# A graph layer's prologue on Trainium2: four groups of four tiles become eight pairs of tiles

## The reference, cut to what matters

```python
h = maximum(layernorm(x), 0)                       # (2048, 256)
type_sum = adj @ h
gate_a = sigmoid(concat([type_sum, h]) @ Wa.T + ba)  # one number per node; gate_b with Wb, bb
g = h @ W_sa
scores = (g @ a_sa[:D])[:, None] + (g @ a_sa[D:])[None, :]
e = where(adj != 0, exp(-leaky_relu(scores, 0.01)), 0)
x_a = e / (e.sum(1) + 1e-5) @ g
x_b = adj @ (h @ W_gcnb) + b_gcnb
return x + sigmoid(gate_a * x_a + gate_b * x_b)
```

## Time and profile before

| what | us |
|---|---|
| median of three runs | 194.56 |
| the profiled execution | 194.4 |
| its span, first to last instruction | 192.6 |
| TensorE busy | 172.1 (89%) |
| VectorE busy | 143.6 (75%) |
| ACT busy | 114.3 (59%) |
| GpSimd busy | 16.1 (8%) |

### The profile page before, as it was taken

How to read it: one execution, slowest core, us unless ns; L and a number is a source line. 1 busy time by engine, 2 the same in 40 slices (tenths; PEclk the granted TensorE clock), 3 DMA queues, 4 the chain that set the end, 5 groups by cost and what they waited for, 6 DMA issues and landing times.

```text
span 192.6 us, 3345 instructions
## 1 busy us (share of the span) xinstructions
PE 172.1 (89%) x1320; PEld 127.0 (66%) x1320; DVE 143.6 (75%) x289; ACT 114.3 (59%) x166; POOL 16.1 (8%) x34
## 2 busy tenths in 40 slices
PE   0348968687999999999999999999999999999993
PEld 0326554455544444588887446888888888888893
DVE  0647574436789999937999993099999999987641
ACT  0285747554489998860947574057587587592421
POOL 1371403302400020000000000000000000000000
PEclk9999999999999999999999999999999999999999
DMA  5999995695000039800000100000001001010210
GB/s 149 404 203 207 213 216 109 109 218 114 3 0 0 0 49 214 175 0 0 3 0 2 58 37 18 0 3 0 0 3 54 0 21 38 2 58 0 93 47 27
DMA packets 3615, 13.72 MB, mean 71 GB/s; under 512 B 400, under 2 KB 784, under 8 KB 2704
## 3 DMA queue, kind: packets, MB, share of 16 engines
q0 software_dynamic: 1296, 8.39, 22.4%
q1 hardware_dynamic: 2016, 4.20, 5.9%
q10 hardware_dynamic: 288, 0.93, 1.4%
HBM read 19.80 MB, written 2.10 MB: 114 GB/s over the span
## 4 chain that ended last, share of the span: by engine, by line
PE 82%; ACT 7%; DMA 3%; DVE 2%; issue 2%; POOL 2%; SPq 0%; DVEq 0%
PE ps L713 23%; PE ps L737 15%; PE ps L738 15%; PE ps L736 15%; PE ps L688 7%; PE ps L729 5%; DMA x_sb<-in_x 3%; ACT scratch L272 3%; PE ps L676 2%; ACT nat_hi L277 1%; ACT scratch L284 1%; PE ps L698 1%; DVE mv_lo L473 1%; DVE scratch L454 1%; ACT mv_hi L295 1%
## 5 line engine op out<-in xcount | busy, mean ns | idle before, releaser
L736 PE MATMUL ps<-mv_lo,e_hi 128*128 128x257 f16 (+2 forms) x272 | 71.0, 267 | 0.0
L738 PE MATMUL ps<-mv_hi,e_lo 128*128 128x257 f16 (+2 forms) x272 | 70.9, 266 | 0.0
L737 PE MATMUL ps<-mv_hi,e_hi 128*128 128x257 f16 (+2 forms) x272 | 70.8, 266 | 0.0
L312 ACT ACTIVATE scratch<-scratch,log_e 128x1024 f32<-128x1024 f32 x32 | 36.7, 1146 | 27.2 <-DVE scratch L499 27.2
L713 PE MATMUL ps<-adj,nat_hi 128*128 128x512 f16 x128 | 48.5, 379 | 0.0
L713 PE MATMUL ps<-adj,nat_lo 128*128 128x512 f16 x128 | 48.5, 379 | 0.0
L499 DVE SCALAR_TENSOR_TENSOR scratch<-sl_row,exs,scratch 128x512 f32<-128x512 f32 x64 | 45.0, 745 | 0.0
L507 DVE TENSOR_TENSOR e_lo<-scratch,e_hi 128x1024 f16<-128x1024 f32 x32 | 39.0, 1219 | 1.2 <-ACT e_hi L320 1.2
L320 ACT ACTIVATE e_hi<-scratch 128x1024 f16<-128x1024 f32 x32 | 33.3, 1041 | 0.0
L737 PEld LDWEIGHTS ps<-mv_hi,e_hi 128*128 128x128 f16 x272 | 26.6, 98 | 3.2
L736 PEld LDWEIGHTS ps<-mv_lo,e_hi 128*128 128x128 f16 x272 | 26.4, 97 | 3.3
(11 more groups left out here) (61 smaller groups left out, 166.4 us busy)
## 6 DMA issues: line engine op xcount, KB each, us to landing
adj<-in_adj_t POOLq DMA_DIRECT2D x7, 1024.0 KB, 12.7
x_sb<-in_x SPq DMA_DIRECT2D x4, 512.0 KB, 7.1
out<-res SPq DMA_DIRECT2D x7, 256.0 KB, 2.0
adj<-in_adj_t POOLq DMA_DIRECT2D x2, 512.0 KB, 7.8
w_sb<-in_weights ACTq DMA_DIRECT2D x1, 518.0 KB, 5.2
c_sb<-in_consts ACTq DMA_DIRECT2D x1, 387.0 KB, 5.9
out<-res SPq DMA_DIRECT2D x1, 128.0 KB, 1.8
out<-res SPq DMA_DIRECT2D x2, 64.0 KB, 1.5
```

The source lines that it names most:

```text
L312: act.activation(z[:, n % ZRING, :, :], z[:, n % ZRING, :, :], ACT.Exp, bias=log_e[:, 0:1], scale=SLOPE - 1.0).then_inc(exp_done, 1)
L736: pe.matmul(ps[:, bank, cols], e_hi[:, s, i1], mv_lo[:, j, cols], start=(j == 0), stop=False)
L737: pe.matmul(ps[:, bank, cols], e_hi[:, s, i1], mv_hi[:, j, cols], start=False, stop=False)
L738: return pe.matmul(ps[:, bank, cols], e_lo[:, s, i1], mv_hi[:, j, cols], start=False, stop=(j == NT - 1))
```

## The change

The prologue goes over eight pairs of tiles (`u`) instead of four groups, and every engine's order is a loop that does the steps of different pairs in turn. TensorE: turn of pair u+1, wide of u, chunk 0's products of pair u. The wide results alternate between banks 2, 3 and 6, 7, the turned pairs between banks 0 and 1. h0 is written over x in place; x is loaded a second time from memory when all turns and low parts are done, for the sum at the end. ACT makes the row scale directly by an exp with a bias, in place of an exp and a GpSimd multiply. x comes in five pieces, the first two of two tiles; all of x, constants and weights are issued by SP; the weights and constants are split in two each, the wide weights ahead of the rest of x. VectorE makes both parts of the wide weights. Sixteen matmuls on zeros stand at the head of TensorE's queue. The turned tiles and the zeros lie in slots of the e ring. The row turns for chunks 2 and 3 go into the middle of chunk 1's products. `half_added` on ACT waits for the second load of x, `agg_highs(0)` stands one step earlier, and the split of the post weights (`w_post_low`) stands between the prologue and the loop on VectorE.

The core of the diff:

```diff
+NU = NT // 2
+WARM = 16
+X_PARTS = ((0, 2), (2, 4), (4, 8), (8, 12), (12, 16))
+WIDE_BANKS = (2, 6)
...
+        h0t_hi = e_hi[:, 16:24, :].rearrange("p (k s) n -> p k (s n)", k=KT)
+        h0t_lo = e_lo[:, 16:24, :].rearrange("p (k s) n -> p k (s n)", k=KT)
+        zeros = e_hi[:, 0, :]
+        z = sb("z", [P, ZRING, 2, CW], F32)
+        far = sb("far", [P, 2, 2, CW], F16)
...
+        def turn_bank(u):
+            return ps[:, u % 2, :].rearrange("p (k n) -> p k n", k=KT)
...
+            def load_x(i):
+                lo, hi = X_PARTS[i]
+                sp.dma_start(x_sb[:, lo:hi, :], x[:, lo:hi, :]).then_inc(x_landed[i], 16)
+
+            load_x(0)
+            load_x(1)
+            sp.dma_start(c_sb[:, :], consts).then_inc(c_landed, 16)
+            sp.dma_start(wa_sb[:, :, :], w_wide).then_inc(wa_landed, 16)
+            for i in range(2, len(X_PARTS)):
+                load_x(i)
+            sp.dma_start(wg_sb[:, :, :], w_post).then_inc(wg_landed, 16)
+            sp.dma_start(r_sb[:, :], rows).then_inc(rows_landed, 16)
+            sp.wait_ge(turned, NU)
+            sp.wait_ge(nat_ready, NU)
             for g in range(NG):
-                sp.dma_start(x_sb[:, g * GT:(g + 1) * GT, :], x[:, g * GT:(g + 1) * GT, :]).then_inc(x_landed[g], 16)
+                ts = slice(g * GT, (g + 1) * GT)
+                sp.dma_start(x_sb[:, ts, :], x[:, ts, :]).then_inc(x_back[g], 16)
...
+            def norms(u):
+                ts = slice(2 * u, 2 * u + 2)
+                pool.wait_ge(var_ready, u + 1)
                 pool.tensor_tensor(rstd[:, ts], var_s[:, ts], power[:, :], ALU.pow).then_inc(rstd_ready, 1)
-                pool.wait_ge(rstd_ready, g + 1)
+                pool.wait_ge(rstd_ready, u + 1)
                 pool.tensor_tensor(shift[:, ts], neg_mean[:, ts], rstd[:, ts], ALU.mult).then_inc(norm_ready, 1)
...
-            pool.wait_ge(x_landed[1], 16)
+            pool.wait_ge(x_landed[0], 16)
             load_adj(0)
             norms(0)
+            norms(1)
             load_adj(1)
-            norms(1)
+            norms(2)
+            norms(3)
             load_adj(2)
+            norms(4)
             load_adj(3)
-            norms(2)
+            norms(5)
             load_adj(4)
-            scales(0)
-            norms(3)
-            scales(1)
+            norms(6)
+            norms(7)
             load_adj(5)
             load_adj(6)
-            scales(2)
-            scales(3)
-            pool.tensor_scalar(column[:, :], factor_r[:, :], MV_SCALE, None, ALU.mult).then_inc(column_done, 1)
+            pool.wait_ge(scales_ready, NU)
...
-            act.dma_start(c_sb[:, :], consts).then_inc(c_landed, 16)
-            act.wait_ge(x_landed[0], 16)
-            act.dma_start(w_sb[:, :, :], weights).then_inc(w_landed, 16)
-
...
+            def h0_tiles(u):
+                act.wait_ge(norm_ready, u + 1)
+                for t in range(2 * u, 2 * u + 2):
+                    act.activation(x_sb[:, t, :], x_sb[:, t, :], ACT.Relu, bias=shift[:, t:t + 1],
                                    scale=rstd[:, t:t + 1]).then_inc(h0_done, 1)
 
...
+            def nat_highs(u):
+                ts = slice(2 * u, 2 * u + 2)
+                act.wait_ge(h0_done, 2 * u + 2)
+                act.activation(nat_hi[:, ts, :], x_sb[:, ts, :], ACT.Copy).then_inc(nat_high, 1)
+
+            def h0t_highs(u):
+                act.wait_ge(turned, u + 1)
+                act.activation(h0t_hi[:, :, 2 * u * P:(2 * u + 2) * P], turn_bank(u),
+                               ACT.Copy).then_inc(h0t_high, 1)
+
+            def mv_highs(u):
+                act.wait_ge(exs_ready, u + 1)
+                act.activation(scale_a[:, 2 * u:2 * u + 2], exs[:, 2 * u:2 * u + 2, SR], ACT.Exp, bias=log_s[:, 0:1],
+                               scale=-SLOPE).then_inc(scales_ready, 1)
+                act.wait_ge(scales_ready, u + 1)
+                for t in range(2 * u, 2 * u + 2):
+                    act.activation(mv_hi[:, t, 0:D], ps[:, WIDE_BANKS[u % 2] + t % 2, 0:D], ACT.Copy,
                                    scale=scale_a[:, t:t + 1]).then_inc(mv_high, 1)
...
+                elif n == 8:
+                    act.wait_ge(wide_product, NT)
...
+                act.wait_ge(x_back[g], 16)
...
+            act.wait_ge(wl_product, 1)
+            act.wait_ge(wa_landed, 16)
+            act.activation(wa_sb[:, :, D:D + 2], wl_bank, ACT.Copy).then_inc(wl_ready, 1)
             h0_tiles(0)
-            act.wait_ge(wl_product, 1)
-            act.wait_ge(w_landed, 16)
-            act.activation(w_sb[:, :, D:D + 2], wl_bank, ACT.Copy).then_inc(wl_ready, 1)
-            act.wait_ge(wl_ready, 1)
-            act.activation(w_hi[:, :, 0:WA], w_sb[:, :, 0:WA], ACT.Copy, scale=W_SCALE).then_inc(w_high, 1)
             h0t_highs(0)
+            h0_tiles(1)
             nat_highs(0)
-            h0_tiles(1)
-            h0t_highs(1)
-            nat_highs(1)
-            factors(0)
-            h0_tiles(2)
-            mv_highs(0)
+            act.wait_ge(consts_ready, 1)
+            for u in range(NU):
+                if u + 1 < NU:
+                    h0t_highs(u + 1)
+                if u + 2 < NU:
+                    h0_tiles(u + 2)
+                if u + 1 < NU:
+                    nat_highs(u + 1)
+                mv_highs(u)
+            act.activation(factor_l[:, :], exs[:, :, SL], ACT.Exp, scale=SLOPE).then_inc(factors_done, 1)
             sl_rows(0)
-            h0t_highs(2)
-            nat_highs(2)
-            factors(1)
-            h0_tiles(3)
-            mv_highs(1)
             sl_rows(1)
-            h0t_highs(3)
-            nat_highs(3)
-            factors(2)
-            mv_highs(2)
-            act.activation(w_hi[:, :, WA:], w_sb[:, :, WA:], ACT.Copy, scale=W_SCALE).then_inc(w_high, 1)
-            factors(3)
-            sl_rows(2)
-            mv_highs(3)
-            sl_rows(3)
-            act.wait_ge(consts_ready, 1)
+            act.wait_ge(wg_landed, 16)
+            act.activation(wg_hi[:, :, :], wg_sb[:, :, :], ACT.Copy, scale=W_SCALE).then_inc(wg_high, 1)
...
+            dve.memset(zeros, 0.0).then_inc(zeros_ready, 1)
+            dve.memset(log_e[:, :], math.log(E_SCALE))
+            dve.memset(log_s[:, :], math.log(MV_SCALE / PROD)).then_inc(consts_ready, 1)
+
+            def moments(u):
...
+            def w_wide():
+                dve.wait_ge(wl_ready, 1)
+                dve.tensor_scalar(wa_hi[:, :, :], wa_sb[:, :, :], W_SCALE, None, ALU.mult).then_inc(wa_high, 1)
+                dve.wait_ge(wa_high, 1)
+                dve.scalar_tensor_tensor(out=wa_lo[:, :, :], in0=wa_sb[:, :, :], scalar=W_SCALE, in1=wa_hi[:, :, :],
+                                         op0=ALU.mult, op1=ALU.subtract).then_inc(wa_ready, 1)
...
-            w_lows(0)
+            w_wide()
             h0t_lows(0)
+            moments(2)
             nat_lows(0)
-            moments(2)
-            narrow_results(0)
-            h0t_lows(1)
-            nat_lows(1)
-            mv_lows(0)
-            moments(3)
-            narrow_results(1)
-            h0t_lows(2)
-            nat_lows(2)
-            mv_lows(1)
-            narrow_results(2)
-            h0t_lows(3)
-            nat_lows(3)
-            mv_lows(2)
-            narrow_results(3)
-            w_lows(1)
-            mv_lows(3)
-            dve.wait_ge(h0t_ready, NG * KT)
-            dve.wait_ge(wide_product, NT)
-            dve.wait_ge(exs_ready, 2 * NG)
+            for u in range(NU):
+                if u + 1 < NU:
+                    h0t_lows(u + 1)
+                if u + 3 < NU:
+                    moments(u + 3)
+                narrow_results(u)
+                if u + 1 < NU:
+                    nat_lows(u + 1)
+                mv_lows(u)
+            w_post_low()
...
+            def turn(u):
+                if u >= 2:
+                    pe.wait_ge(h0t_ready, u - 1)
+                for t in range(2 * u, 2 * u + 2):
+                    pe.wait_ge(h0_done, t + 1)
+                    for k in range(KT):
+                        ins = pe.transpose(turn_bank(u)[:, k, t % 2 * P:(t % 2 + 1) * P], x_sb[:, t, k * P:(k + 1) * P], ident[:, :])
+                ins.then_inc(turned, 1)
...
+            def wide(u):
+                pe.wait_ge(h0t_ready, u + 1)
+                if u == 0:
+                    pe.wait_ge(wa_ready, 1)
+                for t in range(2 * u, 2 * u + 2):
+                    if u >= 2:
+                        pe.wait_ge(mv_ready, t - 3)
+                    for i, (k, a, b) in enumerate(three):
+                        ins = pe.matmul(ps[:, WIDE_BANKS[u % 2] + t % 2, 0:WA], h0t[a][:, k, t * P:(t + 1) * P],
+                                        wa2[b][:, k, :], start=(i == 0), stop=(i == len(three) - 1))
+                    ins.then_inc(wide_product, 1)
...
+            pe.wait_ge(zeros_ready, 1)
+            for i in range(WARM):
```

(20 more changed lines are left out.)

211 lines of the change are left out of this document (82 added, 129 removed).

## The result

The changed kernel took 185.14 us (median of 4 runs, 183.36 to 185.24) beside 194.68 for the kernel before on the same chip (193.88 to 195.0). The ratio is 0.949, with an interval of 0.943 to 0.956: faster by 5%. The forecast was 184.3, in a range from 181.8 to 187.5.

A forecast was written before the change was run, and what follows sets the result against it. TensorE was taken as the bound. Gains of 3.4 (start) and 8.1 (gaps and slow running) less 1.25 (meetings) gave 10.3 us, span 192.6 to 182.3, so 184.3 us median; range 181.8 to 187.5.

The forecast's parts named there:

- What bounds, and the 8.1 us: TensorE bounds; between 15.09 and 80.45 us, 8.1 us are gaps and slow running that the pipeline removes.
- 57.2 us of work: TensorE's work between 15.09 and 80.45 us, summed from the earlier trace's blocks, out of 65.36 us.
- The start: Before the first wide product: it begins at 11.7 us instead of 15.09, a gain of 3.4 us (bounds 1.8 to 4.6).
- The meetings: GpSimd's pow and VectorE's nat_lo block each other in the pipeline: 0.25 us for each of five pairs, 1.25 us lost.
- first rival: Meetings of GpSimd and VectorE cost nothing: 183.0 us, or 182.0 with a better start; chance 0.2.
- The clock: Rival: TensorE's raised clock level is lost before wide(0), costing 1.65, up to 1.9 us: say 185.5; chance 0.2.
- The row that I held against it: Earlier trace, against the lost clock level: a 1.8 us gap ahead of 25.69 left the rate at 0.12.
- The loop: ACT and VectorE's handoff loop in the pipeline takes 3.6 us a pair, exactly TensorE's, with a few tenths of margin.
- third rival: ACT–VectorE loop takes 4.2 us instead of 3.6, or x or adjacency pieces come late: up to 188.0; chance 0.14.
- The covers: Moved transfers and operations stay hidden: x's second load, adjacency pieces, and 8 us of slack for chunk 0's e.
- there near 12: First adjacency piece, issued at 4.5 us, lands near 12, hidden by 1 us before its first product near 13.1.
- 1 to 2: Possible cost in us if the first adjacency piece shares the queues with x.

The follow-up runs named there:

- the three sets: Unaltered changed kernel, four runs each on three chips: medians 185.14, 183.99 and 183.49 us.
- last experiment: Changed kernel with ACT's first h0 and PE's first turn ahead of the weight work, plus later x, post-weight and row loads: 181.61 us, ratio 0.934.
- the memset: Changed kernel plus one 128x512 float32 memset on VectorE in each of the eight pairs: 185.77 us, ratio 0.954.
- the deferred loads: Changed kernel plus nine more matmuls on zeros, with x of tiles 8 to 15, post weights and rows issued after the first h0 tile: 182.23 us, ratio 0.937.
- the early adjacency piece: Changed kernel plus nine zero matmuls and later x, post-weight and row loads, first adjacency piece issued without waiting for x: 185.85 us, ratio 0.954.
- moments in one experiment: Changed kernel with TensorE's turn(u) directly before wide(u) instead of one pair ahead: 199.06 us, ratio 1.020.
- a pow and a DMA issue in another: Changed kernel with the row scale again an exp on ACT and a multiply on GpSimd, per pair: 191.21 us, ratio 0.982.
- the new start: Changed kernel with ACT's first h0 and PE's first turn ahead of the weight work, three zero matmuls behind the small products: 184.25 us, ratio 0.947.

## Why the prediction held, and where it didn't

The forecast of 184.3 lies within the medians of the three sets (185.14, 183.99, 183.49), and the steps that carry the sum held. But two of its terms were wrong, with opposite signs, so that the number is closer than the working deserves.

- *What bounds, and the 8.1 us.* Right. All gaps between 15.09 and 80.45 us are gone, and the time of the changed kernel is TensorE's own work from the first wide product on. The step "57.2 us of work" was 0.7 too high: it takes 2.84 us for 24 wide products from the blocks of the earlier trace rows, and such a block also holds the latency of its last product. The starts lie 0.11 us apart there too (25.69, 25.80). A pair's wide product takes 1.33 us and not 1.42, eight times 0.09.
- *The start.* 11.7 us forecast, 12.31 measured: 2.8 us of gain instead of 3.4. The cause was named rightly (the copy waits for the weights, and the table load behind it). The weights came 0.3 later than the estimate of 6.8, and the two turns ended 0.65 and 0.53 us behind their second h0 tiles instead of 0.4; most of that is the lower level, 0.3 us by the profile in which it held (first wide product at 11.08). The zeros took 6.2 us and ended at 7.35 instead of 6.5; here that was hidden by the weights, in another profile of the same kernel it set the start. The norms were ready at 6.1 instead of 7.0, which is off the path.
- *The meetings, −1.25 us.* Wrong, they cost nothing. The step that failed is "I take 0.25 us for each of the five pairs": the meeting stretches the pow by 0.46 us, and what hangs on the pow is still done 0.1 us before ACT takes it. I had asked whether the two meet and not who waits for the one that is held. This is the first rival (0.2). TensorE has no gap where the level held (last experiment), and the loop doesn't shorten where the meetings are gone (the memset).
- *The clock.* Wrong: I gave the level's loss 0.2, and the mean clock shows it, in full or in part, in 8 of 12 runs. The row that I held against it, 0.12 us spacing after a gap of 1.8 us, followed a long row of products; here eight transposes stood alone. In the profiled run it cost 2.1 us behind the first wide product and about 0.3 ahead of it, where I had said 1.65, up to 1.9. The Trainium skill, page "TensorE: Matmul & The Clock Gate", section "Part 4: PE-mode transpose", says that the full clock doesn't engage for transposes. The trace agrees in so far as the level fell in most runs with eight transposes alone. It doesn't in that a raised level stayed through all eight in one profile (8.30 to 11.08 us, granted clock 1.00), and in four runs at 0.997 and above the mean clock leaves no room for a fall of that length.
- *The two errors.* From the first wide product to the first pair product I had 65.36 − 8.1 + 1.25 = 58.5 us, and 58.8 were measured: +2.1 for the clock, −1.25 for the meetings, −0.7 for the work, 0.1 left over. The profiled span was 1.0 us over the forecast of 182.3; had the meetings not been priced, it would have been 2.3. That these errors cancel is luck.
- *The loop.* 3.6 us worked out, 3.63 measured, and the margin was as thin as said: 0.48 us more on VectorE went into the period whole. The third rival is how this kernel fails next. The range of 181.8 to 187.5 was meant to take it in, but it reaches 188.0 by its own sum.
- *The covers.* x's second load and the slack of 8 us at the first pair product: right. Adjacency piece 0: the step "there near 12" was 2 us too early (9.9 us of transfer instead of 7.3, beside x and the weights); the slow wide product hid it, and where the clock held, it cost 1.16 us, the "1 to 2" that I had put down as a possibility and left out of the sum.

What stays open: why the clock's level holds in some runs over the same instructions and falls in others. No run of the changed kernel in which it held to the end was profiled. With nine more matmuls on zeros it held in three runs of four, with the deferred loads as well in four of four, and with the early adjacency piece in none of four. TensorE's longest wait around the first products was 1.16, 0.1 and 2.80 us in their profiles: the longer the wait, the more runs lost the level, but nothing here varied the wait alone.

## What to carry to other kernels

When a pipeline's loop is about as long as the bound engine's work, work it out handoff by handoff, with all that stands in the same queues: every queued operation between two links belongs to it (moments in one experiment, a pow and a DMA issue in another, each worth several us). For two operations that contend, ask who waits for the one that is held, before giving the meeting a price. And an earlier start is worth only what the next transfer allows: the new start alone brought nothing, and 0.6 us on top of the later loads of x.
